# Attention in an adaLN block: the products with values of two neighbouring key blocks side by side, with eight slots for the softmax's weights

## The chip, the cores and the metric

The kernel runs on one core of a Trainium2 chip. The metric is the time of one execution on the device in microseconds (us). Three runs of the kernel before the change took 997.82, 999.07 and 1000.85 us; the median is 999.07 us.

## What is computed

The reference is one adaLN block on x of shape (4, 1024, 256): a modulation from a conditioning vector, causal attention with 16 heads of 16 features, and a mixture of experts (8 experts, two for each token). Cut to what matters here:

```
h = _layernorm(x, axis=-1) * (1 + ca) + sa
x = x + ga * _L0_attn_ref(h, L0_attn_W_qkv, L0_attn_b_qkv, L0_attn_W_o, L0_attn_b_o)
h = _layernorm(x, axis=-1) * (1 + cb) + sb
x = x + gb * _L0_ffn_ref(h, L0_ffn_gate_w, L0_ffn_w1, L0_ffn_w2)
# inside the attention
scores = jnp.einsum('bhqd,bhkd->bhqk', Q, K) / np.sqrt(D_HEAD)
causal = jnp.triu(jnp.full((t, t), -jnp.inf, dtype=scores.dtype), k=1)
attn = jax.nn.softmax(scores + causal, axis=-1)
O = jnp.einsum('bhqk,bhkd->bhqd', attn, V)
```

The change touches the last line, the products of the softmax's weights with the values.

## The kernel before

**Groups and steps.** The attention is cut into 16 groups (NG), four for each of the four sequences; a group is four heads. A group has 24 steps (NW). The list SCORES names them: for each half f of the queries (512 queries each), for each key block j of 128 keys that the half may see (four blocks for the first half, eight for the second), and for each pair p of the group's four heads. A step makes two scores, one for each head of the pair. Along with them run the row maxima of a later group (34 steps ahead, LEAD): two matmuls a step into a bank of the tile PM (L1600), which VectorE (DVE) reduces (L1319 where the causal mask is in the block, L1322 elsewhere). The maxima are taken off inside the scores' matmul through extra rows of the tile QK. The masked score blocks get a second small matmul (L1627). ScalarE (ACT) turns each score bank into exponentials (L1009), written in float32 to a slot of the tile PR. A slot holds the two heads of one step; there are five (SLOTS).

**Rings.** PS and PM have three PSUM banks each. A score waits until the exponential three scores back is done (L1620), a maximum until the reduction three maxima back is (L1597).

**Products with values.** When both pairs of heads of a key block have their exponentials, TensorE (PE) makes the products with values: the step "pv" of group g, half f, key block j (L1630 to L1646). It is four matmuls, one for each head, with 17 columns of weights: 16 features and a column of ones that gives the softmax's sum. Their outputs stand at partitions 0, 32, 64 and 96 of the one bank PO, so the four heads use four column strips of the array at once. The data are float32, and the trace has two records for each of these matmuls, eight for a set of four. A set covers the queries that may see the block: 512, 384, 256 and 128 columns for the four blocks of the first half; five times 512, then 384, 256 and 128 for the second. So there are twelve sets in a group and 192 in all. PO accumulates over the key blocks of a half; after the last, ACT copies it to OS (L1016), and the first set of the next half waits for that copy (L1638).

**Order.** The function schedule() writes the order of the work out by hand, one list of steps that each engine's program walks through, taking its own part of each step. A set is placed three steps (LAG) behind the step with the second pair of its key block (L226), behind that step's scores and maxima. In group 0 the steps stand further ahead (AHEAD). So on PE two steps of scores and maxima lie between one set and the next. An exponential that reuses a slot waits for the sets that have read it (L1008), counted by the semaphore pv, one for each set.

**Behind the attention.** The weights of the experts are loaded and split on DVE and ACT during the last groups. Then 71 tiles of 128 tokens go through the experts. Their rows are gathered and stored by indirect DMAs of GpSimd (L936, L942), with three buffers XL and four buffers YO.

Of the kernel before, what the change touches and what calls it, by code (L numbers as in the profile page):

```python
# [5 lines left out]
F32 = mybir.dt.float32  # L6
# [4 lines left out]
ACT = mybir.ActivationFunctionType  # L11
# [10 lines left out]
LAG = 3  # L22

WARM = 16
SLOTS = 5

SEGS = ((0, 3), (3, 4))

# [60 lines left out]
def schedule():  # L89
# [124 lines left out]
    for g in range(NG):  # L214
        if g > 1:
            place(g - 2, 2, one("rep", g, 2))
        for f, n in ((2, NM),) if g else ((0, NM0), (1, NM)):
            place(g, n // 2 - LEAD - (f == 0), [(0.5 if g and i else 0, ("cmax", g, f, i)) for i in range(f == 0, 6)]
                  + [(CROW if g else 1 if f == 0 else 2, ("crow", g, f))])
        if g == 0:  # L220
            place(0, NM0 // 2 - LEAD + 3, one("rep", 1, 2))
        if g < NG - 1:
            place(g + 1, LAG + 1, one("od", g))
        for n, (f, j, p) in enumerate(SCORES):
            if p == 1:
                place(g, n + LAG - ahead(g, f), one("pv", g, f, j))  # L226
    for t in range(-3 * nw, NG * nw + LAG + 1):
        now[0] = t - 0.5
# [2 lines left out]
        if 0 <= (t + LEAD) // nw < NG:  # L231
            g, m = divmod(t + LEAD, nw)
# [186 lines left out]
def adaln_block(nc, x, wqkvT, b_qk, b_v, woT, b_o, gate_w, w1, w2, cT, wmod, iota, out):  # L419
    ctx = ExitStack()  # L420

    def sb(name, shape, dt=F32, c=None):
        return (c or ctx).enter_context(nc.sbuf_tensor(name, shape, dt))
# [4 lines left out]
    with ctx:  # L428
# [44 lines left out]
        att = ExitStack()  # L473
# [4 lines left out]
        V = [sb("V0", [128, NT, H, 17], F32, att)]  # L478
        SP = sb("SP", [128, 3, 2, T], BF16, att)
        ZR = sb("ZR", [3, T], BF16, att)  # L480
        QK = sb("QK", [128, 3, 4, 2, T], BF16, att)
        PR = sb("PR", [128, SLOTS, 2, 512], F32, att)
        V.append(sb("V1", [128, NT, H, 17], F32, att))
        OS = sb("OS", [128, 2, T], F32, att)
        JK = sb("JK", [128, 2, 512], BF16, att)
# [14 lines left out]
        BV = sb("BV", [128, 2], F32, att)  # L500
        CS = sb("CS", [128, 2, B], F32, att)
        TM = sb("TM", [128, 2, D], F32, att)
        GBO = TM[:, 0, :]
        WM0 = LP[:, :].rearrange("p (k n) -> p k n", k=2)
        WM1 = OP
# [34 lines left out]
        last = ExitStack()  # L540
# [6 lines left out]
        PS = [ps(f"PS{i}", [128, 512], pat) for i in range(3)]  # L547
        PM = [ps(f"PM{i}", [128, 512], pat) for i in range(3)]
        PO = ps("PO", [128, 512], pat)
# [22 lines left out]
        S = {n: Signal(ctx.enter_context(nc.semaphore(f"s_{n}"))) for n in names}  # L572
# [379 lines left out]
        def scalar_program(eng):  # L952
            ac = Lane(eng)
# [5 lines left out]
            for step in order:  # L959
# [5 lines left out]
                elif kind == "norm":  # L965
                    b, half, i = a
                    ac.wait_ge(*after("rstd", "rstd", 1, b, 15, 2 if b else half))
                    xn_free(ac, step)
                    for n in range(b * NT + 4 * half + 2 * i, b * NT + 4 * half + 2 * i + 2):
                        eng.activation(XN[:, n % 4, :], xt(n, n + 1)[:, 0, :], ACT.Identity, bias=RT[:, n:n + 1],  # L970
                                       scale=RS[:, n:n + 1]).then_inc(S["norm"].sem, 1)
                elif kind == "tr":
# [4 lines left out]
                                   scale=MOD[:, 2 + k, b:b + 1]).then_inc(S["hT"].sem, 1)  # L977
# [23 lines left out]
                elif kind == "score":  # L1001
                    g, n, i = a
                    f, j, pair = SCORES[n]
                    c0, m = 128 * max(0, j - 4 * f), ring_s[step]
                    slot = m // 2 % SLOTS
                    ac.wait_ge(*after("st", *step))
                    if m // 2 >= SLOTS:
                        ac.wait_ge(S["pv"], (m // 2 - SLOTS) // 2 + 1)  # L1008
                    eng.activation(PR[:, slot, i, c0:512], PS[m % 3][:, c0:512], ACT.Exp, scale=0.25).then_inc(S["exp"].sem, 1)  # L1009
                elif kind == "pv":  # L1010
                    g, f, j = a
                    if j == 4 * f + 3:
# [19 lines left out]
                elif kind == "h2":  # L1032
# [3 lines left out]
                    for n in range(b * NT + 2 * tp, b * NT + 2 * tp + 2):  # L1036
                        eng.activation(xt(n, n + 1)[:, 0, :], xt(n, n + 1)[:, 0, :], ACT.Identity, bias=RT[:, n:n + 1],
                                       scale=RS[:, n:n + 1]).then_inc(S["h2a"].sem, 1)
# [469 lines left out]
        def tensor_program(eng):  # L1508
# [25 lines left out]
            for step in order:  # L1534
# [5 lines left out]
                elif kind == "mod2":  # L1540
                    i = a[0]
# [3 lines left out]
                    last = mod_columns(WM1, (256, 384, 512, 640, 0, 128, 768, 896)[i:i + 1], i)  # L1545
# [7 lines left out]
                elif kind == "tr":  # L1553
# [4 lines left out]
                    for j in range(4):  # L1558
                        last = eng.transpose(bank(step)[:, j * 128:(j + 1) * 128], XN[:, j, k * 128:(k + 1) * 128], ident[:, :])
                    last.then_inc(S["px"].sem, 1)  # L1560
                elif kind == "v":
# [4 lines left out]
                    for j in range(2):  # L1566
                        n = 2 * tp + j
                        for k in range(2):
                            last = eng.matmul(bank(step)[:, j * 256:(j + 1) * 256], hT[:, k, n * 128:(n + 1) * 128], W[:, k, 512:768],  # L1569
                                              start=(k == 0), stop=(k == 1))  # L1570
                    last.then_inc(S["px"].sem, 1)
                elif kind == "qk":
# [7 lines left out]
                               stop=True).then_inc(S["px"].sem, 1)  # L1580
# [4 lines left out]
                elif kind == "max":  # L1585
                    g, n = a
                    h, qt, k0, k1, _ = maxima(g)[n]
                    m, r = ring_m[step], slot_of(g)
# [13 lines left out]
                elif kind == "crow":  # L1602
                    g, f = a
# [10 lines left out]
                elif kind == "score":  # L1614
                    g, n, i = a
                    f, j, pair = SCORES[n]
                    c0, m, r, h = 128 * max(0, j - 4 * f), ring_s[step], slot_of(g), 2 * pair + i
# [11 lines left out]
                    last.then_inc(S["st"].sem, 1)  # L1629
                elif kind == "pv":  # L1630
                    g, f, j = a
                    c0 = 128 * max(0, j - 4 * f)
                    n = SCORES.index((f, j, 1))
                    m = ring_s["score", g, n, 1] // 2
                    pe.wait_ge(*after("exp", "score", g, n, 1))
                    pe.wait_ge(*after("v", "v", g // 4, j // 2))
                    if j == 0 and (g, f) != (0, 0):
                        pe.wait_ge(S["os"], S["os"].before[step])  # L1638
                    elif j == 0:
                        pe.wait_ge(S["po0"], 1)  # L1640
                        pe.wait_ge(S["const"], 10)
                    for i in range(4):
                        last = eng.matmul(PO[32 * i:32 * i + 17, c0:512], V[g // 4 % 2][:, j, 4 * (g % 4) + i, :],  # L1643
                                          PR[:, (m - 1 + i // 2) % SLOTS, i % 2, c0:512], start=(j == 0), stop=(j == 4 * f + 3),
                                          skip_group_check=True)
                    last.then_inc(S["pv"].sem, 1)  # L1646
                elif kind == "out":
                    b, tp = a
# [144 lines left out]
```

## Time and profile before

| what | value |
|---|---|
| runs | 997.82, 999.07, 1000.85 us |
| median | 999.07 us |
| span of the profiled execution, first to last instruction | 997.7 us |
| TensorE busy | 902.3 us (90%) |
| VectorE busy | 718.0 us (72%) |
| ScalarE busy | 580.5 us (58%) |
| GpSimd busy | 357.4 us (36%) |
| mean granted TensorE clock | 0.970 |

The profiled execution has no time of its own beside its span; the span lies 1.4 us under the median of the three runs. A matmul is pipelined and its end is modelled, so PE's busy time runs a little over the next start; distances from start to start are the safer reading. PE is the matmuls, PEld the weight loads of the same engine. A granted clock of 1.0 stands for 2.4 GHz, 0.5 for 1.2 GHz.

### The profile page before, as it was taken

To read this page: it belongs to the slowest core of one execution; us is meant where nothing else is said; L and a number is where in the kernel's file an instruction comes from. 1 tells how busy PE (TensorE), PEld (TensorE's weight loads), DVE (VectorE), ACT (ScalarE), POOL (GpSimd) and SP (SyncE) were. 2 spreads that over 40 slices of the span, in tenths; PEclk is the share of its full clock that TensorE was granted. 3 is DMA by queue.
4 is the path that set the end of the run, shared out by engine and by line. 5 is a ranking of instruction groups with operands and counts; after the bars stand their busy time and mean duration, and the time that the engine had idled before them with its cause. 6 is when DMAs were issued, how large, how long until landed. Compare 5 with 4: busy or idle time off the path is not lost.

```text
span 997.7 us, 19445 instructions
## 1 busy us (share of the span) xinstructions
PE 902.3 (90%) x6174; PEld 531.5 (53%) x6174; DVE 718.0 (72%) x2323; ACT 580.5 (58%) x1271; POOL 357.4 (36%) x311
## 2 busy tenths in 40 slices
PE   5899899999899998999999897878899999999990
PEld 3543335433444443543443452423699899999980
DVE  8688766879656789757689669699638584444587
ACT  3335485776585777577666757567535433334562
POOL 1332020431321314333033454015386466565630
PEclk7899899999999999999999999999999999999995
DMA  8446436336326167251662745215313323222699
GB/s 282 127 65 129 61 81 144 59 44 146 63 35 133 42 112 142 69 76 59 106 115 85 152 64 189 73 27 174 96 53 123 95 70 106 78 75 71 198 309 306
DMA packets 83235, 110.61 MB, mean 111 GB/s; under 512 B 15930, under 2 KB 56434, under 8 KB 83138
## 3 DMA queue, kind: packets, MB, share of 16 engines
q1 hardware_dynamic: 75506, 89.45, 38.8%
q0 software_dynamic: 6816, 18.62, 6.1%
q8 instruction: 53, 0.87, 0.4%
q10 hardware_dynamic: 816, 1.32, 0.4%
q14 instruction: 44, 0.36, 0.1%
HBM read 69.42 MB, written 35.41 MB: 105 GB/s over the span
## 4 chain that ended last, share of the span: by engine, by line
PE 62%; DVE 16%; ACT 9%; issue 5%; DMA 4%; POOL 3%; SPq 1%; ACTq 0%; POOLq 0%; DVEq 0%
PE PO L1643 10%; PE PH L1520 9%; PE PY L1520 9%; PE PS L1623 8%; PE PM L1600 8%; ACT PR L1009 4%; DVE MXF L1322 3%; PE PHT L1728 3%; PE PX L1655 2%; PE PX L1569 2%; DVE JK L1319 2%; PE PS L1627 2%; PE PX L1578 2%; PE PX L1579 1%; ACT SF L992 1%
## 5 line engine op out<-in xcount | busy, mean ns | idle before, releaser
L1009 ACT ACTIVATE PR<-PS 128x512 f32<-128x512 f32 (+3 forms) x768 | 334.3, 497 | 142.4 <-PE PS L1627 108.1
L1319 DVE CUSTOM_DVE_ANT_0 JK<-PM,MK 128x128 bf16<-128x128 f32 (+3 forms) x512 | 239.1, 484 | 54.0 <-PE PM L1600 52.8
L1600 PE MATMUL PM<-QK 128*128 128x512 bf16 (+3 forms) x768 | 249.1, 333 | 23.4 <-DVE MXF L1322 15.0
L1623 PE MATMUL PS<-QK 128*128 128x512 bf16 (+3 forms) x768 | 247.5, 333 | 10.4 <-ACT PR L1009 7.4
L1322 DVE TENSOR_REDUCE MXF<-PM 128x1 f32<-128x512 f32 x256 | 175.1, 684 | 83.2 <-PE PM L1600 81.6
L1623 PEld LDWEIGHTS PS<-QK 128*128 128x128 bf16 x768 | 75.0, 98 | 170.4 <-ACT PR L1009 107.8
L1643 PE MATMUL PO<-PR,V 128*17 128x512 f32 (+3 forms) x1536 | 162.8, 496 | 0.0
L1600 PEld LDWEIGHTS PM<-QK 128*128 128x128 bf16 x768 | 75.5, 99 | 98.0 <-DVE MXF L1322 36.8
L1520 PE MATMUL PY<-W2S,HT 128*128 x852 | 118.9, 289 | 2.8 <-issue 1.9
L1520 PE MATMUL PH<-W1S,XT 128*128 x426 | 113.3, 402 | 0.9 <-DVE W2S L1474 0.9
L1627 PE MATMUL PS<-MT,identb 128*128 128x128 bf16 x512 | 111.9, 221 | 0.0
L1072 ACT ACTIVATE HS<-PH 128x512 f32<-128x512 f32 x71 | 42.4, 597 | 114.9 <-PE PH L1520 114.8
L1520 PEld LDWEIGHTS PY<-W2S,HT 128*128 128x128 f32 x852 | 106.0, 189 | 3.5 <-issue 3.4
L942 POOL DMA_INDIRECT YT<-YO,ROW x71 | 75.3, 1061 | 76.0 <-DVE YO L1494 47.8
L1482 DVE TENSOR_TENSOR XT<-PXT,XT 128x256 fp32r<-128x256 f32 x71 | 29.9, 421 | 99.3 <-ACT XT L1066 99.1
L862 POOL TENSOR_TENSOR SF<-SF,SP 128x512 f32<-128x512 f32 x28 | 32.4, 1158 | 179.9 <-ACT SP L999 179.9
L936 POOL DMA_INDIRECT XL<-H2D,TOK x71 | 78.9, 1111 | 48.5 <-PE PXT L1707 21.7
L1520 PEld LDWEIGHTS PH<-W1S,XT 128*128 128x128 f32 x426 | 76.4, 191 | 13.8 <-issue 1.1
L883 POOL TENSOR_TENSOR OP<-OP,LP 128x1024 f32<-128x1024 f32 x7 | 16.5, 2363 | 151.1 <-DVE CP L1343 111.9
L1627 PEld LDWEIGHTS PS<-MT,identb 128*128 128x128 bf16 x512 | 50.5, 99 | 31.1 <-issue 4.6
L1487 DVE TENSOR_TENSOR HT<-PHT,HT 128x512 fp32r<-128x512 f32 x71 | 48.9, 689 | 3.9
L1643 PEld LDWEIGHTS PO<-PR,V 128*17 128x17 f32 x1536 | 25.6, 95 | 34.9 <-issue 26.2
(269 smaller groups left out, 1194.9 us busy)
## 6 DMA issues: line engine op xcount, KB each, us to landing
QK<-SD SPq DMA_DIRECT2D x180, 128.0 KB
SD<-SP SPq DMA_DIRECT2D x42, 256.0 KB, 2.8
OP<-OS SPq DMA_DIRECT2D x64, 64.0 KB
LP<-LR SPq DMA_DIRECT2D x64, 64.0 KB
W1S<-in_w SPq DMA_DIRECT2D x8, 512.0 KB, 5.7
X<-XA SPq DMA_DIRECT2D x3, 1024.0 KB, 8.8
H2D<-XA SPq DMA_DIRECT2D x3, 1024.0 KB, 4.9
YG<-YT SPq DMA_DIRECT2D x12, 256.0 KB, 4.4
```

The lines of the kernel that those rows point to most:

```text
L936: eng.indirect_dma_start(XL[:, t % 3, :], None, H2D[0:(B if t >= NA else B - 1) * T, :], bass.IndirectOffsetOnAxis(ap=TOK[:, t:t + 1], axi ...
L942: eng.indirect_dma_start(YT, bass.IndirectOffsetOnAxis(ap=ROW[:, t:t + 1], axis=0), YO[:, t % 4, :], None, bounds_check=EMPTY - 1 + B * T ...
L1009: eng.activation(PR[:, slot, i, c0:512], PS[m % 3][:, c0:512], ACT.Exp, scale=0.25).then_inc(S["exp"].sem, 1)
L1072: eng.activation(HS[:, t % 2, :], PH[t % 2][:, :], ACT.Silu).then_inc(S["silu"].sem, 1)
L1319: eng.tensor_tensor_reduce(JK[:, jk % 2, 0:w], PM[m % 3][:, 0:w], MK[:, 512 - w:512], 1.0, -3.0e38, ALU.add, ALU.max, MXA[:, mb, h, qt:qt ...
L1322: eng.tensor_reduce(MXF[:, mb, h, qt - 4:qt - 3], PM[m % 3][:, 0:w], AX.X, ALU.max).then_inc(S["mx"].sem, 1)
L1487: eng.tensor_tensor(HT[:, t % 2, 1, :, :], PHT[t % 2][:, :, :], HT[:, t % 2, 0, :, :].bitcast(F32), ALU.subtract).then_inc(S["hlo"].sem, 1)
L1520: last = eng.matmul(out_, stat[:, part, c, :], wt[:, bass.ds(v, 1), c, :].rearrange("p a n -> p (a n)"), start=(j == 0 and c == 0), stop=( ...
L1600: eng.matmul(PM[m % 3][:, 0:128 * (k1 - k0)], QK[:, r, h, 0, qt * 128:(qt + 1) * 128], QK[:, r, h, 1, k0 * 128:k1 * 128], start=True, stop ...
L1623: last = eng.matmul(PS[m % 3][:, c0:512], QK[:, r, h, 1, j * 128:(j + 1) * 128], QK[:, r, h, 0, 512 * f + c0:512 * f + 512], start=True, s ...
L1627: last = eng.matmul(PS[m % 3][:, c0:c0 + 128], identb[:, :], MT[:, :], start=False, stop=True, skip_group_check=True)
L1643: last = eng.matmul(PO[32 * i:32 * i + 17, c0:512], V[g // 4 % 2][:, j, 4 * (g % 4) + i, :], PR[:, (m - 1 + i // 2) % SLOTS, i % 2, c0:512 ...
```

## The change

It leaves out the placing of a set for even key blocks. The set for an odd key block makes the products of the block before it and then its own, eight matmuls in one step of PE, where it used to make four. The position of the odd block's set in the order is as before. The semaphore pv now counts pairs of sets, and the exponentials' wait for a slot is counted accordingly. PR gets eight slots: five where it stood, three in a new tile behind the attention's other tiles. To make room for them, the part of the on-chip memory that holds the descriptors of GpSimd's DMAs is set to 4096 bytes of a partition. Matmuls, their sizes and their data are the same.

```diff
-SLOTS = 5
+SLOTS = 8
+
+
+FIRST_SLOTS = 5
...
         for n, (f, j, p) in enumerate(SCORES):
-            if p == 1:
+            if p == 1 and j % 2:
                 place(g, n + LAG - ahead(g, f), one("pv", g, f, j))
...
-        PR = sb("PR", [128, SLOTS, 2, 512], F32, att)
+        PRA = sb("PRA", [128, FIRST_SLOTS, 2, 512], F32, att)
...
+        PRB = sb("PRB", [128, SLOTS - FIRST_SLOTS, 2, 512], F32, att)
+        PR = [PRA[:, i, :, :] for i in range(FIRST_SLOTS)] + [PRB[:, i, :, :] for i in range(SLOTS - FIRST_SLOTS)]
...
                     if m // 2 >= SLOTS:
-                        ac.wait_ge(S["pv"], (m // 2 - SLOTS) // 2 + 1)
-                    eng.activation(PR[:, slot, i, c0:512], PS[m % 3][:, c0:512], ACT.Exp, scale=0.25).then_inc(S["exp"].sem, 1)
+                        ac.wait_ge(S["pv"], (m // 2 - SLOTS) // 4 + 1)
+                    eng.activation(PR[slot][:, i, c0:512], PS[m % 3][:, c0:512], ACT.Exp, scale=0.25).then_inc(S["exp"].sem, 1)
...
                     g, f, j = a
-                    c0 = 128 * max(0, j - 4 * f)
                     n = SCORES.index((f, j, 1))
                     m = ring_s["score", g, n, 1] // 2
                     pe.wait_ge(*after("exp", "score", g, n, 1))
                     pe.wait_ge(*after("v", "v", g // 4, j // 2))
-                    if j == 0 and (g, f) != (0, 0):
+                    if j == 1 and (g, f) != (0, 0):
                         pe.wait_ge(S["os"], S["os"].before[step])
-                    elif j == 0:
+                    elif j == 1:
                         pe.wait_ge(S["po0"], 1)
                         pe.wait_ge(S["const"], 10)
-                    for i in range(4):
-                        last = eng.matmul(PO[32 * i:32 * i + 17, c0:512], V[g // 4 % 2][:, j, 4 * (g % 4) + i, :],
-                                          PR[:, (m - 1 + i // 2) % SLOTS, i % 2, c0:512], start=(j == 0), stop=(j == 4 * f + 3),
-                                          skip_group_check=True)
+                    for key in (j - 1, j):
+                        c0 = 128 * max(0, key - 4 * f)
+                        for i in range(4):
+                            last = eng.matmul(PO[32 * i:32 * i + 17, c0:512], V[g // 4 % 2][:, key, 4 * (g % 4) + i, :],
+                                              PR[(m - 2 * (j - key) - 1 + i // 2) % SLOTS][:, i % 2, c0:512], start=(key == 0),
+                                              stop=(key == 4 * f + 3), skip_group_check=True)
                     last.then_inc(S["pv"].sem, 1)
...
-    nc = bacc.Bacc("TRN2", target_bir_lowering=False, num_devices=1)
+    nc = bacc.Bacc("TRN2", target_bir_lowering=False, num_devices=1, dynamic_dma_scratch_size=4096)
```

## Rows read from the trace of the kernel before

**Rows 1.** The page's first part: busy us (share of the span) xinstructions of each engine.

```profile
PE 902.3 (90%) x6174; PEld 531.5 (53%) x6174; DVE 718.0 (72%) x2323; ACT 580.5 (58%) x1271; POOL 357.4 (36%) x311
```

**Rows 2.** Windows: stretch, length, busy us of PE, PEld, DVE, ACT, POOL, clock, DMA.

```profile
62.00:702.00 640.00, 591.51 (x4144) 266.13 (x4143) 492.16 (x1721) 427.39 (x954) 179.57 (x141) 0.99 0.45 93
702.00:998.00 296.00, 263.79 (x1828) 238.68 (x1824) 176.60 (x434) 132.96 (x284) 159.94 (x149) 0.96 0.43 133
```

**Rows 3.** Chain by line, 62 to 702 and 142 to 222; L1643's busy PE, PEld.

```profile
by line: PE PO L1643 15.2%; PE PS L1623 12.7%; PE PM L1600 11.5%; ACT PR L1009 5.6%; issue 5.5%; PE PX L1569 3.8%; DVE MXF L1322 3.6%; PE PX L1655 2.8%; DVE JK L1319 2.7%; PE PS L1627 2.6%; PE PX L1578 2.3%; PE PX L1579 2.2%; ACT SF L992 1.
by line: PE PO L1643 22.6%; PE PS L1623 19.9%; PE PM L1600 17.8%; PE PX L1569 8.7%; ACT PR L1009 4.9%; PE PS L1627 3.8%; PE PX L1579 3.2%; PE PX L1578 3.2%; POOL SF L862 2.9%; POOL SP L868 2.9%; ACT SF L992 2.6%; issue 2.4%; DVE MXF L1322 1
62.00:702.00 640.00, 162.39 (x1529) 25.44 (x1530) 0.99 0.45 93
```

**Rows 4.** Waits, 62 to 702: who for whom, us in total, times, longest.

```profile
DVE MXF L1322 <- PE PM L1600: 81.2, 97, 3.7
DVE JK L1319 <- PE PM L1600: 52.0, 62, 2.4
PE PS L1623 <- ACT PR L1009: 7.4, 20, 0.9
```

**Rows 5.** Line L1643: records, ns min/median/max, first and last start, forms.

```profile
L1643 PE MATMUL PO<-PR,V x1536: 272/546/1060, 62.6 to 702.1; 128*17 128x512 f32 x96, 128*17 128x384 f32 x32, 128*17 128x256 f32 x32, 128*17 128x128 f32 x32
```

**Rows 6.** Timeline of PE round two lone sets: start us, us, line, operation.

```profile
300.58 0.22 PE L1600 MATMUL PM<-QK 128*128 128x128 bf16 x1
300.72 1.05 PE L1643 MATMUL PO<-PR,V 128*17 128x512 f32 x8
301.71 0.39 PE L1623 MATMUL PS<-QK 128*128 128x512 bf16 x1
...
288.29 0.41 PE L1643 MATMUL PO<-PR,V 128*17 128x128 f32 x8
288.64 0.39 PE L1623 MATMUL PS<-QK 128*128 128x512 bf16 x1
```

**Rows 7.** Timeline of PE, PEld and ACT at the stage's last two sets.

```profile
701.49 0.92 PE L1643 MATMUL PO<-PR,V 128*17 128x256 f32 x16
702.34 0.33 PE L1706 MATMUL PXT<-ident,XL 128*128 128x128 f32 x1
...
701.49 0.13 PEld L1643 LDWEIGHTS PO<-PR,V 128*17 128x17 f32 x8
701.99 0.13 PEld L1643 LDWEIGHTS PO<-PR,V 128*17 128x17 f32 x8 [0.37 <-ACT PR L1009]
...
701.48 0.46 ACT L1009 ACTIVATE PR<-PS 128x128 f32<-128x128 f32 x2 [0.71 <-PE PS L1627]
```

**Rows 8.** Timeline of PE, DVE and ACT round one set of 512 columns.

```profile
306.81 1.05 PE L1643 MATMUL PO<-PR,V 128*17 128x512 f32 x8
...
307.64 0.08 DVE L1319 DVE_READ_ACCUMULATOR2_ANT MXA<- 128x1 f32 x1
308.34 0.56 DVE L1319 CUSTOM_DVE_ANT_0 JK<-PM,MK 128x384 bf16<-128x384 f32 x1 [0.61 <-PE PM L1600]
...
308.17 0.93 ACT L1009 ACTIVATE PR<-PS 128x256 f32<-128x256 f32 x3 [1.08 <-PE PS L1627]
```

**Rows 9.** Groups by form: xcount, busy us, mean ns, idle us before and its releasers.

```profile
L1009 ACT ACTIVATE PR<-PS 128x512 f32<-128x512 f32 x384 | 207.0, 604 | 74.7 <-PE PS L1627 42.2 <-PE PS L1623 31.6
L1322 DVE TENSOR_REDUCE MXF<-PM 128x1 f32<-128x512 f32 x256 | 175.1, 684 | 83.2 <-PE PM L1600 81.6
```

**Rows 10.** Windows, columns as in rows 2: three stretches with DVE busiest.

```profile
220.00:260.00 40.00, 35.09 (x261) 14.60 (x260) 36.60 (x136) 25.02 (x59) 7.26 (x6) 1.00 0.47 104
380.00:420.00 40.00, 36.23 (x275) 18.45 (x272) 36.49 (x167) 26.98 (x62) 13.93 (x11) 1.00 0.58 130
660.00:702.00 42.00, 37.43 (x318) 13.46 (x315) 38.47 (x74) 29.84 (x72) 16.45 (x11) 0.97 0.41 119
```

**Rows 11.** GpSimd's DMAs: the queue, the stores' issue, us to landing.

```profile
q0 software_dynamic: 6816, 18.62, 6.1%
...
L942 POOL DMA_INDIRECT YT<-YO,ROW x71 | 75.3, 1061 | 76.0 <-DVE YO L1494 47.8 <-ACT YO L1085 23.0 <-issue 3.7
...
YT<-YO,ROW POOLq DMA_INDIRECT x71, 2.7
```

## The prediction, made before the changed kernel was run

> **What bounds the kernel now.** I read the engines' busy line first [rows 1]: TensorE (PE) is busy nine tenths of the span, VectorE (DVE) seven, ScalarE (ACT) under six. Then the windows by stage [rows 2]: the products with values run from 62 to 702 us, and there PE is busy 591.5 of 640 us, DVE 492.2, ACT 427.4. The stage behind it has none of the changed steps. Third, the chain of work that ended last, cut to the stage [rows 3]: the line of the products with values (L1643, tile PO) carries 15.2% of 640 us, 97 us, the scores 12.7%, the matmuls for the maxima 11.5%. So PE is the bound, but not everywhere: all lines of PE together are well short of the whole, and the waits [rows 4] show DVE standing 81.2 + 52.0 us for matmuls of the maxima, while PE stands only 7.4 us for an exponential. Whatever shortens PE's own work in this stage shortens the kernel, as long as DVE and ACT get their input in time.
>
> **What one set costs PE.** A set is four heads' products for one key block. There are 1536 matmul records on the line [rows 5], eight for a set, so 192 sets, twelve a group: 96 of 512 columns, 32 each of 384, 256 and 128 (the counts of that row). The timeline of PE [rows 6] shows two lone ones. The set of 512 columns starts at 300.72 and the next ordinary matmul starts at 301.71: 0.99 us. The set of 128 columns goes from 288.29 to 288.64: 0.35 us. The difference of 0.64 us for 384 columns makes 0.213 us for 128, and what is left at no columns is 0.99 - 0.85 = 0.13 us. That is a fixed cost behind each set. There is one ahead of it too: the matmul of 128 bf16 columns at 300.58 needs 0.05 us (a quarter of 0.213, if the float32 set makes four passes, as its price per column says), so the set could begin at 300.63 and begins at 300.72: 0.09 us. A set thus costs 0.13 + 0.09 = 0.22 us over its streaming.
>
> **What is joined.** The diff puts two sets side by side, so 96 of the 192 pairs of edges go. What the seam costs instead has one witness, the last two sets of the stage, which have no score between them already [rows 7]: they start at 701.49, the next matmul at 702.34, 0.85 us for 384 columns, less 0.64 of streaming: 0.21. Less the 0.13 behind a set that leaves 0.08 for the seam, as an upper end. The second set's weight loads start at 701.99 after 0.37 us that the profile puts down to ACT, whose last two exponentials ended at 701.94. So most of the 0.08 is that wait, and the lower end is 0. I take 0.02, since inside a set the second four weight loads cause no visible stop: all eight are over 0.13 us after the set's start [rows 7], while the first four matmuls are still streaming. A joined pair saves 0.20 us (bounds 0.14 and 0.22). Of 96 pairs the last one is joined already, so 95 count: 19.0 us of PE time (13.3 to 20.9).
>
> The Trainium skill, "TensorEngine Tiling (Array Packing)", Key Properties, says that changing the tiling mode drains the engine; by that rule the 0.22 us is the drain, and the trace agrees. The same skill, "TensorE: Matmul & The Clock Gate", Part 3, says that weight loads overlap running matmuls only where the row group differs. All four heads use all 128 rows, so by that rule the seam would be paid in the open; the eight loads within 0.13 us speak against it. What it would make of the sum is rival C.
>
> **What of it reaches the end.** PE is busy 162.4 us with these sets in the stage, and the chain runs through them for 97 us [rows 3]. I take that ratio, 0.60: 19.0 x 0.60 = 11.4 us. The ends are 19.0 (all of it) and nothing.
>
> **What the change adds.** First, a longer hole for the engines behind PE. A long pair (1024 or 896 columns; two and two of the six in a group, 64 in all) holds PE for 1.71 + 0.02 + 0.22 = 1.95 us (896 columns: 1.73) where the longest hole was 1.08. [Rows 8] show a hole as it is: the set starts at 306.81, DVE works off its queue until 307.73, gets its next maximum at 308.34 and stands 0.61 us; ACT stands 1.08. A bank of PM holds one maximum, there are three, so DVE has at most three queued, 3 x 0.68 = 2.05 us [rows 9]. From a long pair's start to the next filled bank it takes 1.53 + 0.87 = 2.40 us (the distance in [rows 8] plus the second set), 2.19 with 896 columns. DVE stands at least 0.35 or 0.14 us, and 0.61 + 0.87 = 1.48 with the queue of [rows 8]. Where DVE has slack in the period this costs nothing: the mean is 133 us of standing over 96 periods, 1.4 us each [rows 4]. Where it has none, it goes into the time. [Rows 10] show such stretches: DVE is busy 36.6 of 40 us at 220, 36.5 of 40 at 380, 38.5 of 42 at 660. They are 122 of 640 us, so 18 of 96 pairs, 12 of them long. I price each at 0.30 us, between the two least holes and nearer the larger, because a full queue is what a tight stretch has and DVE's other operations stand in it too: 12 x 0.30 = 3.6 us. Bounds: 0 if those fill the hole, 12 x 1.48 = 18 us if the queue is as short as in [rows 8].
>
> Second, ACT. Its hole grows from 1.08 to 1.95 us, but a pair's period holds eight exponentials of at most 0.54 us (the wide ones' busy time by their count [rows 9]), 4.3 us, in 640 / 96 = 6.7 us. I take nothing. If that cover fails, PE's 7.4 us of standing for ACT doubles: +7.4.
>
> Third, slots. With eight slots the exponential of pair P needs the set of pair P - 8, placed two steps ahead of it in PE's order where it was one before, so the added wait is never the late one; the wide exponentials stood 74.7 us, of which 42.2 + 31.6 went to the scores' two lines and nothing of note to the sets [rows 9], so the three slots buy nothing either. PE's wait for the exponentials stays three steps behind the later key block. The wait for the copy of PO moves to two steps later: nothing. What is queued behind a joined pair on PE is two steps of scores and maxima, which is the hole above; on ACT, the copy of PO at the end of a query half, at the same place as before.
>
> Fourth, the end of the stage. In [rows 7] the set of 256 columns (2 x 0.213 = 0.43 us) ran while ACT finished; joined it waits too: 0.43 us, on the path, once.
>
> Fifth, the scratch of GpSimd's DMA descriptors is cut to 4096 bytes. The indirect transfers carry 6816 packets in 142 of them, 48 each, three on an engine [rows 11], and by the buffers XL and YO three gathers and four stores are the most in flight. I take nothing; the bound is a rival.
>
> **The sum.** The profiled execution's span is 997.7 us; the median of the three runs is 999.07, 1.4 us above, with what lies outside the span. -11.4 + 3.6 + 0.4 = -7.4 us: 990.3 in the span, 991.7 in the time.
>
> **The rivals.**
> A. All of it passes, because the stretches where PE wasn't in the chain were late for reasons that PE sets too. For it: from 142 to 222 us the line carries 22.6% of the chain, 18.1 us, nearly all of that stretch's 24 sets at a mean of 0.64 + 0.13 us [rows 3]. Against it: the mean over the stage. 999.07 - 19.0 + 0.4 = 980.5.
> B. DVE's holes give the gain back. A third of the pairs are tight, 21 long ones at 0.45 us: 9.5. 11.4 - 9.5 - 0.4 = 1.5: 997.6. For it: DVE is busy 492 of 640 us, and the shorter the period, the more so.
> C. Weight loads at the seam in the open: 0.13 us each. A pair saves 0.09, 95 make 8.6, 0.60 of it 5.1, less 4.0: 998.0. Against it: all eight loads of a set are over while the first four matmuls stream [rows 7].
> D. Slower, by starved DVE. The mechanism is the three banks of PM: no more than 2.05 us of maxima can be queued, and a long pair needs 2.40. If half of the pairs are tight, 32 long ones cost 14.4 us at 0.45, the other half of the joins brings 5.7, and the tail costs 0.4: 999.07 + 9.1 = 1008. It outweighs the gain from some 25 tight long pairs on, where 0.45 each makes 11.4. Against it: the mean slack of 1.4 us; for it: that the slack is uneven, with long holes beside the projections.
> E. The smaller scratch makes each indirect transfer wait for the one before. A landing takes 2.7 us [rows 11]; 142 of them, with 1.06 us of issue, make 534 us in a stage of 296: 238 us more, 1237. Against it: three packets an engine.
>
> **How the numbers follow.** Forecast (986 to 996) 0.50; A 0.12; B 0.19; C 0.04; D 0.12; E 0.03. About 0.3%, 3 us, is what a measurement of this kernel can tell from no change: faster is forecast and A, 0.62; within 0.3% B and C, 0.23; slower D and E, 0.15. The range is 983 to 1002: it takes the forecast, the nearer half of A, B and C, and a little of D, and leaves out two in ten.
>
> **What would show it.** In the changed kernel's trace: sixteen records of PO side by side, 96 times, and a pair of 1024 columns from its start to the next matmul in 1.86 us (1.92 and above if the seam is in the open). The stage from the first set to the last about 7 us shorter, the stage behind it the same 296 us. DVE's standing behind long pairs near 1.5 us at slack places, its sum for the stage no larger than 133 us; if the sum grows, B or D is at work, and PE's own waits for DVE and ACT will have grown too. ACT's waits for PE fewer and longer. The forecast is wrong if these grow by more than 11 us together, or if the stage behind the products changes.

## The result and the profile after

The changed kernel takes 1009.90 us (median of 4 runs, 1007.98 to 1011.03) where the kernel before takes 998.92 (with a fourth run beside the three above). The ratio is 1.0112, with a 95% interval of 1.0091 to 1.0132: 11 us slower. The forecast was 7.4 us faster. The result lies outside the range, beside rival D.

The page of the changed kernel: busy us and share of the span (1009.0 us) of each engine, then its chain.

```profile
PE 895.9 (89%) x6101; PEld 538.5 (53%) x6174; DVE 710.0 (70%) x2323; ACT 577.4 (57%) x1271; POOL 357.9 (35%) x311
PE 60%; DVE 16%; issue 8%; ACT 8%; DMA 3%; POOL 2%; SPq 2%; another core or an unknown queue 1%; DVEq 0%; ACTq 0%; POOLq 0%
```

PE has fewer matmul records (6101 for 6174) because 73 are missing from this trace; its weight loads are complete. A wait that such a matmul ended is put down to "remote" or "issue" below.

Windows, in the columns of [rows 2]: the stage of the products with values, now 12 us longer, and the stage behind it.

```profile
62.00:714.00 652.00, 585.99 (x4083) 273.55 (x4153) 485.80 (x1722) 424.37 (x956) 179.76 (x141) 0.98 0.45 92
714.00:1009.00 295.00, 263.22 (x1816) 238.23 (x1814) 175.03 (x432) 132.96 (x284) 160.22 (x149) 0.96 0.42 134
```

All of the loss is in the first. The last set started at 702.1 [rows 5] and starts at 713.6 now, 11.5 us later. The stage behind it takes 295 us for 296.

**The seam.** The timeline of PE and PEld at a joined pair of 1024 columns.

```profile
344.72 0.61 PE L1649 MATMUL PO<-PRA,V 128*17 128x512 f32 x2
344.74 0.61 PE L1649 MATMUL PO<-PRB,V 128*17 128x512 f32 x2
345.16 0.60 PE L1649 MATMUL PO<-PRA,V 128*17 128x512 f32 x2
345.18 1.46 PE L1649 MATMUL PO<-PRB,V 128*17 128x512 f32 x10
346.56 0.34 PE L1628 MATMUL PS<-QK 128*128 128x384 bf16 x1
...
345.16 0.12 PEld L1649 LDWEIGHTS PO<-PRB,V 128*17 128x17 f32 x4 [0.31 <-issue]
345.59 0.12 PEld L1649 LDWEIGHTS PO<-PRB,V 128*17 128x17 f32 x4 [0.31 <-issue]
```

Sixteen records in a row, and 1.84 us from the pair's start to the next matmul (346.56 - 344.72). Two single sets take 2 x 0.99 us and an entry of 0.09 between them, 2.07. So the pair saves 0.23 us by these rows, all of the 0.22 that was worked out for two edges; the seam costs nothing that can be seen. The two lines of PEld show how: four weight loads of the second set run at 345.16, beside the second half of the first set's matmuls, and four at 345.59, beside the first half of its own. No group of matmuls waits for them: the four groups start at 344.72, 345.16, 345.59 and 346.02. PE was given its 21 us (95 x 0.22).

**Where they went.** Waits in the stage, 62 to 714 us: who for whom, us in total, times, longest.

```profile
DVE MXF L1327 <- PE PM L1605: 64.8, 59, 2.8
DVE JK L1324 <- PE PM L1605: 57.7, 59, 4.0
DVE MXF L1327 <- remote: 28.9, 17, 5.8
PEld PM L1605 <- DVE MXF L1327: 42.6, 97, 1.7
PEld PM L1605 <- DVE MXA L1324: 28.4, 69, 1.5
```

The same waits of PEld in the kernel before, 62 to 702 us, and those of the matmuls behind them, which the prediction did not use:

```profile
PEld PM L1600 <- DVE MXF L1322: 33.1, 66, 2.1
PEld PM L1600 <- DVE MXA L1319: 16.4, 34, 1.6
PE PM L1600 <- DVE MXF L1322: 14.5, 23, 1.9
PE PM L1600 <- DVE MXA L1319: 6.6, 15, 1.1
```

Both sides of PM's three banks stand longer. DVE stands 64.8 + 57.7 + 28.9 = 151 us for maxima, where it was 133 [rows 4]. The weight loads of the maxima stand 71 us at a full ring, where it was 49.5. DVE has the same operations to do as before. So the ring is full at one time and empty at another, and more so than before; that it is too short for the rhythm of its two ends is the reading that the experiments below put to the test.

A load's idle time is not time lost by PE: part of it runs while the matmul before still streams. The matmuls' own waits for these banks are 21.1 us before and 23.5 after (13.6 + 9.9), though the matmuls missing from this trace can hide some. ACT's side shows how far the loads' row can be from a loss: the loads of the scores wait 107.8 us for ACT before and 36.8 + 17.9 us after, though the kernel is slower; much of it is the 0.85 us behind a set of 512 columns, while that set streams. So these sums are signs, not prices. Pair by pair, in the records of the 64 long pairs: behind 50 of them, from the pair's start to 1.5 us after its end, DVE stands over 0.35 us; ahead of 36, since the set before, loads of maxima wait over 0.1 us for a reduction; 28 have both. In the kernel before DVE stands so behind 62 of the 96 single sets of 512 columns, so the holes are not new; they are longer, 1.1 us on average behind a long pair and 0.55 behind such a set.

One period shows both. First PEld ahead of the pair of 344.72, then DVE and ACT round it.

```profile
343.36 0.10 PEld L1605 LDWEIGHTS PM<-QK 128*128 128x128 bf16 x1 [0.37 <-DVE MXF L1327]
344.37 0.10 PEld L1605 LDWEIGHTS PM<-QK 128*128 128x128 bf16 x1 [0.36 <-DVE MXF L1327]
...
344.67 0.69 DVE L1327 TENSOR_REDUCE MXF<-PM 128x1 f32<-128x512 f32 x1
345.28 0.55 DVE L1324 CUSTOM_DVE_ANT_0 JK<-PM,MK 128x384 bf16<-128x384 f32 x1
345.75 0.21 DVE L1355 COPY CT<-PX 96x128 bf16<-96x128 bf16 x1
347.21 0.69 DVE L1327 TENSOR_REDUCE MXF<-PM 128x1 f32<-128x512 f32 x1 [1.25 <-remote]
...
343.08 1.89 ACT L1014 ACTIVATE PRA<-PS 128x512 f32<-128x512 f32 x4
346.99 1.48 ACT L1014 ACTIVATE PRA<-PS 128x384 f32<-128x384 f32 x4 [2.02 <-PE PS L1632]
```

Ahead of the pair the ring is full: the loads of two maxima wait 0.37 and 0.36 us for reductions (idle time of the loads; a part of it runs while PE still streams). Then the pair holds PE. DVE has two reductions and a copy left, is done at 345.96 and stands 1.25 us; ACT stands 2.02. Below, the kernel before round the same two key blocks, whose sets there start at 340.19 and 342.78: DVE behind each of them, and the only load between 338.5 and 344.5 us that waits at PM's ring.

```profile
341.82 0.69 DVE L1322 TENSOR_REDUCE MXF<-PM 128x1 f32<-128x512 f32 x1 [0.43 <-PE PM L1600]
344.31 0.56 DVE L1319 CUSTOM_DVE_ANT_0 JK<-PM,MK 128x384 bf16<-128x384 f32 x1 [0.61 <-PE PM L1600]
...
342.57 0.10 PEld L1600 LDWEIGHTS PM<-QK 128*128 128x128 bf16 x1 [0.19 <-DVE MXF L1322]
```

There DVE stands 0.43 + 0.61 us, 0.2 less than behind the pair, and the loads wait 0.19 us where they wait 0.73 ahead of it. In this period the larger difference is on PE's side: the maxima that it can't place before the pair. From start to start PE itself loses 0.21 and 0.25 us there (a masked score's matmul of 0.05 us of streaming at 343.10 and 344.08, the maxima's matmuls at 343.36 and 344.38). It is one period; the sums above are the stage's.

### The profile page after: what moved, and what is told of

The parts are those of the page before. It is cut to its first block, busy times and chain, and to the rows that moved or that the text cites. A ratio compares the mean times of both kernels' runs of the same rounds, so it can differ in the third digit from the quotient of the medians.

```text
span 1009.0 us, 19277 instructions
## 1 busy us (share of the span) xinstructions
PE 895.9 (89%) x6101; PEld 538.5 (53%) x6174; DVE 710.0 (70%) x2323; ACT 577.4 (57%) x1271; POOL 357.9 (35%) x311
## 4 chain that ended last, share of the span: by engine, by line
PE 60%; DVE 16%; issue 8%; ACT 8%; DMA 3%; POOL 2%; SPq 2%; another core or an unknown queue 1%; DVEq 0%; ACTq 0%; POOLq 0%
PE PO L1649 10%; PE PH L1525 10%; PE PY L1525 10%; PE PM L1605 6%; PE PS L1628 6%; DVE JK L1324 4%; DVE MXF L1327 4%; ACT PRA L1014 3%; PE PHT L1734 3%; PE PX L1574 2%; PE PX L1661 2%; PE PX L1583 2%; PE PX L1584 2%; DMA LD<-OS 1%; SPq L700 1%
## 5 line engine op out<-in xcount | busy, mean ns | idle before, releaser
L1014 ACT ACTIVATE PRA<-PS 128x512 f32<-128x512 f32 (+2 forms) x480 | 226.9, 552 | 71.5 <-PE PS L1632 60.9
L1605 PE MATMUL PM<-QK 128*128 128x512 bf16 (+3 forms) x726 | 233.9, 330 | 30.1 <-DVE MXF L1327 14.5
L1628 PE MATMUL PS<-QK 128*128 128x512 bf16 (+3 forms) x737 | 236.9, 330 | 15.4 <-ACT PRA L1014 7.9
L1014 ACT ACTIVATE PRB<-PS 128x128 f32<-128x128 f32 (+2 forms) x288 | 107.8, 416 | 78.5 <-PE PS L1632 51.9
L1649 PE MATMUL PO<-PRA,V 128*17 128x512 f32 (+2 forms) x960 | 123.7, 548 | 1.0 <-DVE MXF L1327 0.5
L1649 PE MATMUL PO<-PRB,V 128*17 128x128 f32 (+2 forms) x576 | 58.7, 414 | 0.0
```

Of the source, the lines that this page charges most:

```text
L1014: eng.activation(PR[slot][:, i, c0:512], PS[m % 3][:, c0:512], ACT.Exp, scale=0.25).then_inc(S["exp"].sem, 1)
L1605: eng.matmul(PM[m % 3][:, 0:128 * (k1 - k0)], QK[:, r, h, 0, qt * 128:(qt + 1) * 128], QK[:, r, h, 1, k0 * 128:k1 * 128], start=True, stop ...
L1628: last = eng.matmul(PS[m % 3][:, c0:512], QK[:, r, h, 1, j * 128:(j + 1) * 128], QK[:, r, h, 0, 512 * f + c0:512 * f + 512], start=True, s ...
```

## The experiments

Each is compared with the kernel before on the same chip. Two theories went in: that the loss comes from the three-bank rings between PE and its two consumers (banks), and that it comes from something else the change brought, above all the slots, the scratch or the joined step itself (placement). Where an experiment relieves an engine, the kernel before gets the same edit as its counterpart.

**1. The joining undone.**

```diff
+SETS = {(f, j): (j,) for f in range(2) for j in range(4 * f + 4)}
...
-            if p == 1 and j % 2:
+            if p == 1 and (f, j) in SETS:
...
-                    for key in (j - 1, j):
+                    for key in SETS[f, j]:
```

The slots and the scratch of the change stay; the exponentials' wait is counted by single sets.

> The changed kernel with the joining undone: twelve sets a group again, each three steps behind its key block; the eight slots and the smaller descriptor scratch stay. Banks theory (the long hole of a joined pair, 1.84 us for 1024 columns where a single set has 0.99, empties the three banks of PM and of PS, and what DVE and ACT stand then is paid back by PE at the full rings): 999 us as before the change, within 2 us, since slots and scratch carry nothing. Rival, placement (the extra slots behind the other tiles or the small scratch slow the exponentials or the transfers): 1008 to 1010 us, the whole loss stays.

Measured: 998.23 us, ratio 0.9995 (0.9970 to 1.0021). Slots, tiles and scratch cost and bring nothing that can be seen. The 11 us are the joining's, which makes the even block's products later as well as putting them side by side with the odd block's; experiments 12 and 13 part the two.

**2. and 3. Only the short, only the long pairs.** Both differ from experiment 1 in one line, the first and the second below. The first joins the sets of 256 and 128 columns at the end of each half (32 pairs), the second those of 1024 and 896 columns together (64 pairs); the other sets are single.

```diff
+SETS = {(f, j): (j - 1, j) if j == 4 * f + 3 else (j,) for f in range(2) for j in range(4 * f + 4) if j != 4 * f + 2}
...
+SETS = {(f, j): (j - 1, j) if j < 4 * f + 2 else (j,) for f in range(2) for j in range(4 * f + 4) if j % 2 or j == 4 * f + 2}
```

> Joined are only the two sets of 256 and 128 columns at the end of each query half, 32 pairs of 96; the other sets stand alone; eight slots. Banks theory: the joined pair holds PE for 0.78 us, less than a single set of 512 columns (0.99), so no hole is longer than before, and 32 seams save 0.22 us each, 7.0 us of PE time, of which some 0.6 passes: 995 us (992 to 998). Rival, that any joining loses because the first block's products come two steps later: 32/96 of the loss of 11 us, 1003 us.

> Joined are only the pairs of 1024 and 896 columns, 64 of 96; the sets of 256 and 128 columns stand alone. With the short pairs joined alone nothing was lost or won (998.8). Banks theory: only pairs whose hole is longer than a single set's lose, so all of the loss is here: 1007 to 1011 us. If losses went by the number of pairs: 1003 to 1006 us.

Measured: 998.81 us for the short ones, ratio 1.0004 (0.9988 to 1.0020); 1009.84 for the long ones, ratio 1.0111 (1.0067 to 1.0155). The long pairs carry the whole loss, as the banks theory has it. But its gain for the short ones, 4 us, did not come either. Waits of that kernel hint at what took it:

```profile
PEld PM L1609 <- DVE MXF L1331: 39.8, 93, 1.7
PEld PM L1609 <- DVE MXA L1328: 26.1, 55, 1.6
```

66 us at full banks of PM over the whole run, where the kernel before has 36.8 + 18.9 = 56. The short pairs stand where the score blocks are narrow; that PE is quick there, and waits for DVE what it saves, fits but was not tested. The sum is no measure of the loss: the kernel with the long pairs joined has 40.9 + 26.5 = 67 us in the same two rows, no more, and is 11 us slower.

**4. to 9. Each consumer relieved.** DVE: the reductions read the first half of their columns.

```diff
-                        eng.tensor_reduce(MXF[:, mb, h, qt - 4:qt - 3], PM[m % 3][:, 0:w], AX.X, ALU.max).then_inc(S["mx"].sem, 1)
+                        eng.tensor_reduce(MXF[:, mb, h, qt - 4:qt - 3], PM[m % 3][:, 0:w // 2], AX.X, ALU.max).then_inc(S["mx"].sem, 1)
```

The masked reduction is cut in the same way. ACT: the exponentials write the first half of their columns, from group 1 on.

```diff
-                    eng.activation(PR[slot][:, i, c0:512], PS[m % 3][:, c0:512], ACT.Exp, scale=0.25).then_inc(S["exp"].sem, 1)
+                    c1 = (c0 + 512) // 2 if g else 512
+                    eng.activation(PR[slot][:, i, c0:c1], PS[m % 3][:, c0:c1], ACT.Exp, scale=0.01).then_inc(S["exp"].sem, 1)
```

> The changed kernel with half of DVE's work on the row maxima: each reduction reads the first half of its block's columns only, and the exponentials' scale is 0.01 in place of 0.25 so that they stay finite (the maxima aren't the true ones, the weights aren't the softmax's). PE's work is the same. To be compared with the kernel before with the same edit. Banks theory, if PM's ring is the main one: PE's waits for DVE (50 us in the changed kernel, 36 before) nearly vanish in both, the pair saves its 21 us of drains and loses only what ACT's ring costs (12 us more): 955 to 970 us, 5 to 15 us under its counterpart. If ACT's ring is the main one, still at or above its counterpart. Placement rival: 11 us above its counterpart.

> The kernel before the change with half of DVE's work on the row maxima (each reduction reads the first half of its block's columns, the exponentials' scale is 0.01). Banks theory: 999 less most of the 36 us that PE waited for PM's banks: 965 to 978 us. If DVE weren't a bound anywhere, 999.

> The changed kernel with both rings relieved: the reductions of the maxima read the first half of their columns, and from group 1 on the exponentials write the first half of theirs (scale 0.01; the rest of a slot keeps old values, so the weights aren't the softmax's). PE's work is the same. Banks theory: with both consumers light neither ring is full when a joined pair begins nor dry long enough to matter, so the 96 seams at 0.22 us, 21 us of PE time, come through nearly whole: 12 to 20 us under its counterpart, some 945 to 955 us. Rival, that joined sets lose in another way (projections and other work of PE come later behind a long pair): no more than 5 us under its counterpart.

> The kernel before the change with the same two edits (reductions over half the columns; exponentials over half from group 1 on, scale 0.01). It is the counterpart: 975 us, as with DVE relieved alone, less up to 13 us that PE waited for the scores' banks: 962 to 970 us.

> The changed kernel with ACT relieved alone: from group 1 on the exponentials write the first half of their columns (scale 0.01; not the softmax's weights), the reductions are whole. So far the changed kernel stands 11 us above its counterpart with both rings loaded, level with it with DVE relieved, 7 us under it with both. If the two rings' shares add up, ACT's share is 7 to 8 us: 3 to 4 us above its counterpart. If DVE's ring alone costs all that joining costs while it is loaded: 9 to 11 us above.

> The kernel before the change with ACT relieved in the same way: 999 less what PE waits for the scores' banks, 988 to 996 us.

Measured, in us (ratio to the kernel before with its interval):

| relieved | joined | not joined | joined less not joined |
|---|---|---|---|
| nothing | 1009.90 (1.0091 to 1.0132) | 998.92 | +11.0 |
| DVE | 975.40 (0.9735 to 0.9778) | 974.55 (0.9719 to 0.9769) | +0.9 |
| ACT | 1002.41 (0.9998 to 1.0051) | 997.58 (0.9946 to 1.0000) | +4.8 |
| both | 961.26 (0.9585 to 0.9673) | 968.38 (0.9627 to 0.9746) | -7.1 |

A number of the last column is good to 2 (nothing), 3 (ACT) and some 6 us (DVE, both) by the scatter of the runs beside it, so the steps between the rows are sizes, not exact shares. Relieving DVE takes away about 10 us of what joining costs, relieving ACT about 6, both together 18; within these errors the two add up. With both relieved, joining is a gain, 7 us and just clear of its error, of the 21 us that the drains are worth. In the kernel with DVE relieved, DVE's waits are long and PE's short, as they should be:

```profile
DVE MXF L1327 <- PE PM L1605: 135.2, 106, 4.1
PEld PM L1605 <- DVE MXF L1327: 14.2, 23, 4.4
PEld PM L1605 <- DVE MXA L1324: 10.9, 24, 1.3
```

25 us at PM's full banks in place of 77 over the whole of the changed kernel's run. For ACT alone 3 to 4 us above was expected and 4.8 came. The expectations for the joined kernels with DVE relieved (955 to 970) and with both (945 to 955) were too low: I had let too much of the 21 us through. The experiments vary the consumers' work, never the number of banks: that both consumers carry the loss is shown, that three banks are too few for it is worked out from the sizes.

**10. and 11. The products over half of their columns.** DVE and ACT are loaded as in the two kernels, only the sets are short.

```diff
-                        c0 = 128 * max(0, key - 4 * f)
+                        c0 = (256 + 64 * max(0, key - 4 * f)) if g else 128 * max(0, key - 4 * f)
```

> The changed kernel with the products with values over half of their columns from group 1 on (the other half of PO keeps old values; the exponentials' scale is 0.01; the output isn't the attention's). DVE and ACT have all of their work, the joining and its seams are unchanged, only the hole is shorter: 0.99 us for 1024 columns cut to 512, the length of a single set in the kernel before. Banks theory: a hole of that length costs little, as in the kernel before, and most of the saved 21 us is kept where PE is the bound; but with half the products DVE is nearer to being the bound: 2 to 10 us under its counterpart. Rival, that it is the joining and not the hole's length: 9 to 11 us above its counterpart.

> The kernel before the change with the products over half of their columns from group 1 on (scale 0.01). Counterpart of the run above: the 115 us of streaming in those groups are halved, 57 us of PE time, of which some 0.6 passes: 955 to 970 us.

Measured: 978.86 us joined (ratio 0.9781, 0.9731 to 0.9830), 972.80 not joined (0.9732, 0.9690 to 0.9774). The gain that I expected (2 to 10 us under the counterpart) isn't there; the joined kernel stands 6 us above, by intervals that overlap, so that it loses is likely and not shown. Its longest hole is 0.99 us where the single sets leave 0.56. The kernel without joining missed its expectation too (955 to 970). What changed with the sets is the bound, as the waits of the kernel without joining suggest, over its whole run:

```profile
PEld PM L1600 <- DVE MXF L1322: 46.8, 93, 2.7
PEld PM L1600 <- DVE MXA L1319: 27.7, 48, 4.1
```

That is 74.5 us at PM's banks where the kernel before has 56. It fits that half the products leave DVE in front, so that PE's saving has nowhere to go. This run does not decide between a hole's length and the bunching of the work between holes.

**12. and 13. Moved, not joined.** Twelve sets a group, both edges of each paid, but the even block's set stands later: 0.5 step or 1 step ahead of the odd block's, where it is 2 in the kernel before. The edit is on top of experiment 1's.

```diff
-                place(g, n + LAG - ahead(g, f), one("pv", g, f, j))
+                place(g, n + LAG + 1.5 * (j % 2 == 0) - ahead(g, f), one("pv", g, f, j))
```

The other has 1 for 1.5.

> Twelve sets a group, none joined, eight slots, but the even key block's set is moved to half a step before the odd one's: one score and one maximum stand between the two. Both edges of every set are paid. If the position is what costs (the hole's length and the bunching together, one half step short of the changed kernel's), it loses what the changed kernel loses before its seams pay anything back: DVE's and ACT's shares, 10 and 6 us, less a little for the one maximum in between, 1008 to 1018 us. If something in the joined step itself costs, 999 us.

> The same with the even block's set one whole step before the odd one's: two scores and two maxima between them, six behind. By the position theory between the two others: 1001 to 1008 us, nearer to 1001 since two maxima feed DVE for 1.2 us of the second set.

Measured: 1005.47 us at half a step, ratio 1.0066 (1.0042 to 1.0089); 1004.01 at one step, ratio 1.0036 (1.0013 to 1.0059). One of the ten runs at half a step took 3027 us, for no reason that is known; without it the median is 1004.76. The position alone costs: nothing is joined here, and there is a loss of 4 to 6 us. At one step it is as expected, at half a step smaller than the 1008 to 1018 expected; perhaps the maximum that still reaches DVE between the sets is worth more than I gave it. Joined outright the loss is 11 us although the drains are saved. The two distances can't be told from each other.

**14. and 15. The maximum ahead of the score.** The order of the two kinds in every half step is turned round, in the changed kernel and in the kernel before.

```diff
-        if score:
-            order.append(("score", *score, 1))
         order += fill[1:]
+        if score:
+            order.append(("score", *score, 1))
```

The first half step likewise.

> The changed kernel with the order on PE turned round in every half step: the maximum's matmul, then the score's, where it was score, then maximum. All of the work is there. Banks theory: behind a joined pair DVE gets its next maximum 0.2 to 0.7 us sooner, because no score and no mask stand before it, and ACT its next score by as much later. DVE is the fuller of the two, so the loss shrinks: 1000 to 1006 us. If the banks weren't the cause, 1010 us.

> The kernel before the change with the same turned order. Single sets leave DVE almost no hole, so little is to be had: 996 to 1001 us by the banks theory; slower where ACT's input comes later.

Measured: 1005.94 us joined (ratio 1.0075, 1.0038 to 1.0112), 1002.10 not joined (1.0022, 1.0003 to 1.0042). With the maximum ahead of the score DVE should get its work sooner behind a pair. The joined kernel stands 4 us under the changed kernel; the kernel without joining has no such long hole and loses 2 to 3, just above the 996 to 1001 expected. The gap between the two shrinks from 11 to 4 us (good to 2) with no work taken away. It fits the rings and nothing in the joined step itself. No version with all of the work beats the kernel before.

## Why the prediction was wrong

**The cost of a set's two edges** was right: 0.22 us. **The seam** was given 0.02 us and costs less than the rows can show, so a pair saves 0.22 to 0.23, not 0.20. Its last witness, the 0.08 us between the stage's last two sets [rows 7], was ACT's exponential, as said. **Rival C** is out: by the timeline above, weight loads for all 128 rows overlap matmuls that use all 128 rows. The Trainium skill, "TensorE: Matmul & The Clock Gate", Part 3, says in its list of what overlaps that they do so only where the row group differs; the trace disagrees (loads at 345.16 us, matmuls on the same rows streaming from then to 345.59), and the measurement decides. The mechanism told at the head of that Part of the Trainium skill also lets a load into the background weight buffer overlap, and the trace fits that; the prediction did not weigh it. The Trainium skill's page "TensorEngine Tiling (Array Packing)", Key Properties, says that a change of tiling mode drains the engine; the 0.22 us that joining removes agree with it.

**What reaches the end**, 0.60 of what PE is freed by, was too high. A share of the chain says where PE is late now, not that it stays the late one when it is made faster. The 11.4 us of gain can't be measured alone. The short pairs freed 32 x 0.22 = 7 us and brought 0 where the ratio gave 4. Even with both consumers relieved it was 7 of 21, a third.

**The cost of the longer hole** is the step of the prediction that failed: 12 tight pairs at 0.30 us, 3.6 us, for DVE, and nothing for ACT. The runs with the consumers relieved show some 18 us in its place, about 10 for DVE and about 6 for ACT (each good to some 5). The mechanism was named, its cost was mis-sized: with 18 for 3.6 the forecast's own sum is 7 us slower in place of 7.4 faster. Whether the count or the price was wrong is not shown. With the forecast's gain of 11.4 us kept, the loss of 11 asks for 22 us over the 64 long pairs, 0.34 each, near the 0.30 if every one is tight; DVE's 10 alone are 0.16 a pair. That DVE stands behind 50 of the 64 in the changed kernel's trace, and that loads of maxima wait ahead of 36, speaks for many more tight pairs than 12 and against all of them. I had read tightness from DVE's busy share in windows of 40 us [rows 10] and from its mean standing of 1.4 us a period [rows 4]. Slack in another part of the window is hard to use: three banks carry 2 us of work, and a pair's whole period is 6.7 us. A warning was in the trace: DVE's 133 us of standing and, in the same stage, 49.5 us of PEld's and 21.1 us of PE's own waits at PM's full banks. I read the first, and of PE's side only the 7.4 us for ACT.

**ACT** was taken at nothing because of a cover, 4.3 us of exponentials in 6.7, that is again a mean, and its ring has three banks too.

**The signs** that the prediction named for B or D came: DVE's standing for maxima grew from 133 to 151 us, and PE's own waits for DVE and ACT at the two rings from 28.5 to 33.4.

**Slots, placement, scratch, the stage behind:** nothing, as said (998.23 us with all three in and the joining out; rival E is out). **Rival D** named the mechanism and gave 1008 for the 1009.9 measured, with half of the long pairs tight at 0.45 us, nothing for ACT and a gain of 5.7; that its number is so near is in part luck. It had a chance of 0.12.

**What stays open:** how the loss divides between the length of the hole and the bunching of eight scores and maxima without a break, since experiments 10 to 13 change both or change the bound; where the other 14 of the 21 us go when both consumers are relieved; and whether the depth of the rings is what has to be longer. No run has more banks or fewer: PS, PM, PO and PX take three, three, one and one, and none was given up for a fourth bank of PM.

## What to carry to other kernels

An engine that feeds others through a short ring must not only be fast but even: before its work is bunched, compare the longest time that it is away, from its last product to its next, with what the ring holds in the consumer's time (here 2.4 us against three reductions of 0.68). If the producer waits for full slots and the consumer for work in the same stage, suspect that time freed on the producer will mostly turn into waiting; a busy share over a long window hides this. Look for the producer's waits at its weight loads as well as at its matmuls, but don't price them by the loads' idle time: here 66 us of it went with no loss and 67 with 11 us. What prices them is a run with the consumer made lighter, beside its counterpart without the change.

## What the runs showed of the hardware

Column-tiled float32 matmuls follow each other with no visible stop across two sets of weights: a pair of 1024 columns takes 1.84 us, 0.13 above its streaming of 1.71, which is what a single set of 512 has. Half of the second set's weight loads (four at 345.16 us) run under the matmuls of the first and the other half (345.59) beside its own, although all use all rows of the array. The stops of 0.09 us ahead of a set and 0.13 behind it are paid once for two sets side by side.
